# A two-step round in the order of TensorE's work, with the value products of both steps at its end

## The reference

```python
xn = layernorm(x)
qkv = xn @ w_qkv + b_qkv                 # 16 heads of 16 features
scores = where(j >= i, q @ k.T / 4, -inf)
s = softmax(scores) @ v                  # per head, then all heads together
s = s @ w_out + b_out
h = concat([xn, -xn]);  h = relu(s0 * h @ sign(k0)) * 2    # 1024 features
h = relu(s1 * h @ sign(k1)) * 2                            # 1024 features
g = silu(s2 * h @ sign(k2))                                # 256 features
out = x + s * g
```

## Time and profile before

| what | before |
|---|---|
| median of 3 runs | 2318.76 us |
| the profiled execution | 2317.55 us |
| its span | 2315.8 us |
| mean granted TensorE clock | 0.986 |
| PE busy | 2230.2 us (96%) |
| DVE busy | 1811.5 us (78%) |
| ACT busy | 1580.9 us (68%) |
| POOL busy | 915.3 us (40%) |

### The profile page before, as it was taken

How to read it: one execution, slowest core, us unless ns; L and a number is a source line. 1 busy time by engine, 2 the same in 40 slices (tenths; PEclk the granted TensorE clock), 3 DMA queues, 4 the chain that set the end, 5 groups by cost and what they waited for, 6 DMA issues and landing times.

```text
span 2315.8 us, 60916 instructions
## 1 busy us (share of the span) xinstructions
PE 2230.2 (96%) x23760; PEld 1539.8 (66%) x23760; DVE 1811.5 (78%) x4516; ACT 1580.9 (68%) x3199; POOL 915.3 (40%) x1080
## 2 busy tenths in 40 slices
PE   7997999999999999999999999999999999999985
PEld 6786776666666666677666666666666666666652
DVE  7774787888888878788888878788888787888722
ACT  5662466777777777777777677677777776776662
POOL 1003534333433534344453445343443544354433
PEclk9998999999999999999999999999999999999997
DMA  8984111111111313131121223131322212132221
GB/s 299 359 317 167 39 29 40 43 50 46 47 49 35 94 40 87 48 86 51 51 83 45 81 59 83 41 90 43 83 55 53 83 44 84 50 83 69 81 92 58
DMA packets 157844, 193.31 MB, mean 83 GB/s; under 512 B 65276, under 2 KB 102076, under 8 KB 157560
## 3 DMA queue, kind: packets, MB, share of 16 engines
q1 hardware_dynamic: 156600, 189.41, 27.2%
q10 hardware_dynamic: 960, 0.00, 0.0%
HBM read 112.13 MB, written 76.14 MB: 81 GB/s over the span
## 4 chain that ended last, share of the span: by engine, by line
PE 84%; DMA 6%; DVE 4%; SPq 2%; issue 1%; ACT 1%; POOL 1%; POOLq 0%; ACTq 0%; DVEq 0%
PE b_ps L1406 25%; PE b_pv_ps L1372 22%; PE b_ps L1343 15%; PE b_ps L1353 12%; PE b_ps L1402 5%; DMA a_xs<-L_attn_x 4%; PE b_ps L1427 3%; DVE a_stats L397 1%; DVE a_qk_parts L435 1%; ACT b_u L1492 1%; DVE b_part_max L1518 1%; SPq L113 1%; PE b_ps L1360 1%; SPq L1186 0%; PE a_qk_ps L291 0%
## 5 line engine op out<-in xcount | busy, mean ns | idle before, releaser
L1461 ACT ACTIVATE b_probs<-b_ps 128x512 f32<-128x512 f32 (+3 forms) x2560 | 1258.4, 538 | 563.8 <-PE b_ps L1343 533.7
L1518 DVE TENSOR_REDUCE b_part_max<-b_ps 128x1 f32<-128x512 f32 x1536 | 972.4, 681 | 184.0 <-PE b_ps L1353 177.2
L1353 PE MATMUL b_ps<-k_kst,k_qst 48*128 48x512 f32 (+3 forms) x2560 | 896.3, 391 | 8.7 <-DMA k_kst<-qk_parts 3.4
L1343 PE MATMUL b_ps<-k_qst,k_kst 50*128 50x512 f32 (+3 forms) x2560 | 891.7, 389 | 11.7 <-DMA k_qst<-b_max_parts 11.1
L1343 PEld LDWEIGHTS b_ps<-k_qst,k_kst 50*128 50x128 f32 x2560 | 431.9, 185 | 323.7 <-DVE b_part_max L1518 115.8
L1515 DVE CUSTOM_DVE_ANT_0 b_ps<-b_ps,k_mask 128x512 f32<-128x512 f32 (+3 forms) x1024 | 483.5, 513 | 153.8 <-PE b_ps L1353 147.1
L1372 PE MATMUL b_pv_ps<-b_probs,k_vst 128*32 128x512 f32 (+3 forms) x5120 | 597.5, 541 | 0.5 <-POOL b_probs L1247 0.2
L1406 PE MATMUL b_ps<-b_u_hi,k_w 64*128 64x256 f32 x4096 | 590.0, 281 | 2.1 <-ACT b_u L1492 1.1
L1406 PE MATMUL b_ps<-b_u_lo,k_w 64*128 64x256 f32 x4096 | 588.5, 280 | 0.0
L1353 PEld LDWEIGHTS b_ps<-k_kst,k_qst 48*128 48x128 f32 x2560 | 432.9, 185 | 137.6 <-DVE b_part_max L1518 43.5
L1406 PEld LDWEIGHTS b_ps<-b_u_hi,k_w 64*128 64x128 f32 x4096 | 460.7, 187 | 20.2 <-ACT b_z L1483 4.2
(11 more groups left out here) (105 smaller groups left out, 1922.6 us busy)
## 6 DMA issues: line engine op xcount, KB each, us to landing
qk_parts<-a_qk_parts SPq DMA_DIRECT2D x64, 512.0 KB, 3.9
k_kst<-qk_parts SPq DMA_DIRECT2D x384, 64.0 KB, 2.3
k_qst<-qk_parts SPq DMA_DIRECT2D x384, 64.0 KB, 2.3
a_xs<-L_attn_x SPq DMA_DIRECT2D x16, 512.0 KB, 6.0
xn_T<-a_xT SPq DMA_DIRECT2D x16, 512.0 KB, 5.7
v_plain<-a_v_out SPq DMA_DIRECT2D x16, 512.0 KB, 5.4
k_xf<-xn_T SPq DMA_DIRECT2D x32, 256.0 KB, 3.2
b_v_in<-v_plain SPq DMA_DIRECT2D x64, 128.0 KB, 2.6
```

The lines of the kernel that those rows point to most:

```text
L1343: pe.matmul(dst[:, 0:cols], keys, qst[rows, c, pair, 0:cols], start=True, stop=True).then_inc(s_ready, 1)
L1353: pe.matmul(dst[:, 0:CHUNK - k1], qst[rows, c, pair, i * P:(i + 1) * P], kst[rows, k_slot(kc, g % 2), pair, k1:CHUNK], start=True, stop=Tr ...
L1461: act.activation(probs[:, s % P_SLOTS, h, 0:cols], ps[:, banks[place, 0][0], 0:cols], ACT.Exp, scale=HD ** -0.5).then_inc(exp_done, 1)
L1518: dve.tensor_reduce(dst, src, AX_X, ALU.max).then_inc(ring_read, 1)
```

## The change

Two constants of `Plan` change. The round has two steps' worth of R (eight letters) with three F between them, and two V at its end. A V out of turn needs 4 waiting steps instead of 2.

```diff
     SLACK, QUANTUM = 60, 1
-    ROUND = "RRFRRV"
-    EARLY = 2
+    ROUND = "RRFRRFRRFRRVV"
+    EARLY = 4
```

## The result

The changed kernel takes 2351.46 us, the median of 4 runs (2350.88 to 2354.49), against 2318.57 for the kernel before beside it: ratio 1.0141, 95% interval 1.0125 to 1.0158, 33 us slower. The forecast was 2354. Its total is nearly exact and its parts are not: two terms were too large by half or more, and a third, put at nothing, is about 24 us.

What follows compares the result with a forecast made beforehand. The prediction took PE to bound the kernel: 2317.55 us, less 40 for passages saved, plus 82 for idle time added, gave 2359.6, shaded to 2354 us. Its own range was 2325 to 2390 (0.52); 2268 to 2402 with 2 in 10 left out.

Steps and rivals of the forecast that it cites:

- What bounds the kernel: PE sets the time: idle 10.3 us in the 1600 from 400 to 2000 us, DVE at 82.5%.
- The passage: PE's switch between divisions of its array, to V and back: 0.33 us extra, once per block of V's.
- Term 1: Passages saved on PE: 131 of 320 rounds keep their pair, 500 blocks, 121 x 0.33 = 40 us less.
- Term 2: PE idle where F is unavailable: starts 96 us (0.6 each), swaps 16, less about 30 already planned: +82 us.
- The swaps: PE's idle time at the 160 swaps of F's banks: 160 x 0.1 = 16 us.
- Parts at nothing: F letters, depth of probs, transposes and projections, SP's and POOL's queues, first stage and tail: no time added to the sum.
- The sum: Whole kernel: 2317.55 - 40 + 82 = 2359.6 us, shaded to 2354 us.
- much slower: Rival: starts nearly always go without a V, 2480 us; 2400 where starts idle 1 us each; chance 0.10.
- more than 120 double places: Sign in PE's timeline: V blocks of 16 instructions in 120 to 150 places, before 16.
- PE's idle time of 50 us or more from 400 to 2000 us: Sign: PE's idle rises from 10 to 50 us or more, in gaps of 0.2 to 0.6 us between SM's.
- DVE's idle time before L1518: Sign at DVE's line L1518: its idle time there comes with longer single waits.
- under 20 us and I am wrong: Refuting sign: PE idle under 20 us from 400 to 2000 us; the time then goes to the faster rival, chance 0.27.

Runs made afterwards that it cites:

- e3: Kernel before with the new round and EARLY = 5, so nearly no V goes out of turn (328 blocks): 2380.36 us, ratio 1.0257.
- e4: Kernel before with EARLY = 5 and a round ending RVRV, one SM between the two V's (637 blocks): 2445.07 us, ratio 1.0530.
- the five orders of the table: Change, all pairs, new round alone, two new V rules, all with later gate stores, against the kernel before with them: +8.6, +47, +31, -13, -13 us.
- e5: Changed kernel with only SP's queue altered, the gate's store up to 60 entries later: 2318.80 us, ratio 0.9991 to the kernel before.
- e6: Kernel before with only SP's queue altered, the gate's store up to 60 entries later: 2311.24 us, ratio 0.9954.
- e11: Kernel before with the new round, EARLY = 5 and SP's gate stores later (328 blocks): 2357.61 us, ratio 1.0156 to the kernel before.

## Why the prediction was right, and where it was wrong

- *What bounds the kernel*: right. Every order is set by what PE does not do; DVE never became the bound (busy for 82.6% before and 81.0% after, from 400 to 2000 us), and the test with split pairs excludes starved readers as the loss.
- *The passage, 0.33 us*: right, 0.29 to 0.33 by e3 against e4, and 0.34 by the five orders of the table.
- *Term 1, -40 us*: right in kind, too large. 96 double blocks and not 131, 541 blocks and not 500, so -26 us. The step that failed is the share of rounds that keep their pair, 4.1 in 10: it is 3 in 10. 428 of the 640 V's go out just when the fourth waiting step is complete, and after such a V none is left over for a pair. One of its premises was misread: with the 202 V's at a V letter, not 342 but 438 of the kernel before are out of turn, 424 of the 640 in times in which F is unavailable.
- *Term 2, +82 us*: right in kind and sign, more than twice too large. The planned waits grew by 45 us, and +35 is what the 8.6 us between e5 and e6 leave when the blocks are taken at 0.33: 0.78 of the planned. The mis-sized quantity is the idle time per start, 0.6 us or 96 in all: the order plans 59.6 us at the 160 starts, 0.37 us each, and nothing at 43 of them. The swaps were right, 19.0 us against 16. Why a start waits so little was not tested.
- *Parts at nothing, "SP's and POOL's queues get the same issues in the same places by step"*: wrong, and the one mechanism that the forecast lacked, +24 us. The issues are the same in number, but not in order: finished uses of F move against the steps, and in POOL's queue 12 gate products fell behind one more of them. A queue that works in order also carries the time at which each wait ends. The gate's store waits for POOL at the network's pace, the loads behind it are needed at the maxima's pace, and the new order moved one against the other: at 640 us the store came 12 us later where the masks ahead of it came 5.5 us later. In the kernel before such waits were there already: 231.6 us of SP at that line. Of PE's 8.2 us in gaps over 1 us, 5.8 are gone when the store is moved (e6).
- *The sum*: -26 + 35 + 24 = +33; it closes by construction, since the 35 is a remainder, and what supports its split is that the same prices fit the other orders. The forecast's -40 + 82, shaded to +36, hit the total by luck: the overestimated waits stood in for late loads that it did not have. The sign did rest on the right argument: without the late loads the change still loses, by 8.6 us. The size did not. In the rival *much slower*, 1 us of idle per start gives 2424 us by the prediction's own terms (+160 + 16 - 30 - 40), not 2400.
- *The signs to look for*: more than 120 double places: no, 97 blocks with more than one V. PE's idle time of 50 us or more from 400 to 2000 us: no, 23.4, of which most are the few long gaps; the short waits lie inside the matmuls' modelled lengths. DVE's idle time before L1518 hardly changed, 185.9 us against 184.0. The limit "under 20 us and I am wrong" was a bad meter, and only distances between starts would have served.

## What to carry to other kernels

A filler is worth most where nothing else can run. Before grouping work to save the cost of changing over, count how much of it stands in such places, price both in the same unit (here 0.33 us per change against 0.8 us per us of planned wait), and group only what those places don't need. When an order changes, walk down every in-order queue, of the compute engines too, and ask of each wait whose pace ends it and who needs what stands behind it: a store of results ahead of loads can cost more than the change itself.

## What the runs showed of the hardware that was not expected

A long gap of PE costs more than its length. In the changed kernel the granted clock went to the 1.2 GHz level in the idle gaps of 3.84, 4.75 and 7.23 us and stayed there for 10.2, 6.8 and 6.8 us, beyond their ends. The first matmuls behind the last two (PE, in brackets the idle time ahead):

```profile
1917.10 0.76 PE L1353 MATMUL b_ps<-k_kst,k_qst 48*128 48x512 f32 x1 [4.75 <-issue]
```

```profile
2053.88 0.76 PE L1353 MATMUL b_ps<-k_kst,k_qst 48*128 48x512 f32 x1 [7.23 <-issue]
```

They take 0.76 us where the same form takes 0.40 in the median. Two shorter gaps of the changed kernel, of 1.61 and 2.90 us, came with 3.4 and 6.8 us at that level too (from 1.2 us behind the end of the first, and from within the second), two of 1.56 and 1.48 us with none. The short waits were hardly followed by it: e11 has 164 gaps of 0.02 to 0.92 us with 33 us in all and 3.4 us at the lower level from 300 to 2200 us, the changed kernel 7 longer gaps with 23.4 us and 34.1 us at the lower level.
